# Score matmuls in four visits of four heads on four banks, values and denominators together, VectorE's steps in other slots

## The chip, the cores and the metric

One core of a Trainium2 chip runs the whole kernel. The metric is the device time of one execution in microseconds (us).

## The reference

The input x (32 batches of 256 tokens, 256 features) passes three blocks, each followed by a residual and a norm. The first, four layers of a recurrence, takes the first 2150 us and isn't touched. The second and third are "the second stage":

```python
q, k, v = heads(x @ Wq), *heads(context @ Wkv)          # 16 heads of 64
sim = clip(where(mask, q k^T * SCALE, -max), -5, 5)
x = layernorm(x + softmax(sim) v @ Wo + bo)
gate = silu(bitlinear(x, w_gate)); up = bitlinear(x, w_up)
x = layernorm(x + bitlinear(gate * up, w_down))         # INNER 1024
# bitlinear: activations rounded to 127 steps of the row's maximum, weights to -1, 0, 1
```

Ahead of them the first block's output gets its norm, is added to x and normed again: this is "the norm of the later batch" below (`x1_...`), since it is made two batches ahead.

## The kernel before, in words

`attend_and_feed` is the second stage. Each engine has its own instruction list, written out by hand in a loop over the 32 batches `j`; they meet at semaphores alone. PSUM has eight banks of 128 x 512 float32. In batch `j` the engines make the attention of `j`, the feed-forward of batch `f = j - 1`, and on VectorE the norms of batch `later = j + 2`.

TensorE's list for a batch: twelve `unit`s (L844, L851: the projections to k, q and v, in a high and a low half-precision part; 8 to 11 are v), with `transpose_x` and `feed_in` of `f` between them; `scores(j, pair)` (L866: two heads, six matmuls of 64 rows each, the two heads side by side in the array). Then four quads `q` of four heads: `attend(j, q, half)` (L876: values, 32 columns at a time), `denominators(j, q)` (L888), `out_project` (L920), and once a batch `x1_features(j + 1)` (L911), `transpose_h(f)` (L957), `feed_out(f)` (L966).

Who serves the scores: VectorE clips each head from PSUM to `scores` (`clip`, L1184); ACT exponentiates (`exps`, L1036); POOL adds the two halves of the keys (`add_halves`, L780), and among these additions splits the context of batch `j + 2` (`context_split`, L766, L768) after the fourth and makes `attended_lo` (L784). `denominators` sums over partitions; ACT takes logarithm and reciprocal (`denominators`, L1080, L1082); VectorE multiplies (`attended`, L1269); ACT makes the high part (`attended_hi`, L1089), POOL, or in the last quad VectorE (`last_attended_lo`, L1276), the low part, for `out_project`.

VectorE has besides: `h_max`, `h_steps`, `h_round_up` (L1236), `h_round_down` (L1240), which quantise the hidden values of `f` in two tiles of 128 tokens; `fed` (L1282) and the sum `x_plus_attended` (L1472). For the later batch it has `x1_moments(later, 0)` (L1296, L1299), `x1_centre` (L1305), `x1_residual` (L1314), `x1_moments(later, 1)`, `x1_second_norm` (L1324). After each pair of moments ACT makes the reciprocal deviation: `x1_rstd` (L1093, L1095), which in ACT's list of quads 2 and 3 stands right ahead of `denominators(j, q)`:

```python
                for q in range(QUADS):
                    for i in range(4 * q + 4, 4 * q + 8):
                        if i == 4 * q + 6:
                            if q > 1 and later:
                                x1_rstd(later, q - 2)
                            denominators(j, q)
                        if i < AHEADS:
                            exps(j, i)
```

`h_features` (L1059) on ACT copies the transposed hidden values for `feed_out`. Three banks (0 to 2) hold scores, 3 and 4 values and denominators (and units), 5 the output, 6 and 7 the feed-forward and the transposed `x1`.

## Time and profile before

| | us |
|---|---|
| median of 3 runs (lowest to highest) | 3659.48 (3659.18 to 3664.34) |
| the profiled execution | 3659.03 |
| its span | 3657.3 |
| TensorE busy, matmuls | 3537.8 (97%) |
| VectorE busy | 3376.8 (92%) |
| ACT busy | 3049.9 (83%) |
| POOL busy | 2178.4 (60%) |

Busy time on TensorE counts matmuls whose ends are modelled, so that 97% is not 97% of what the array can do. The span has two parts: up to 2148 us the recurrence, then the second stage. An engine's list runs strictly in order, so the time at which an instruction starts is set by the one ahead of it or by the last semaphore that it waits for; the views in order of time show which, in brackets behind the row.

### The profile page before, as it was taken

The page shows a single profiled execution, that of the slowest core. Times are in us where ns is not written, and L with a number is a line of the kernel's source. Part 1 is how long each engine was busy: PE and PEld are TensorE (multiplying, and loading weights), DVE is VectorE, ACT ScalarE, POOL GpSimd, SP SyncE. Part 2 cuts the span into 40 slices and gives each one's busy share as a digit, 9 for nine tenths or more (in the row PEclk, how much of TensorE's full clock was granted, in tenths as well). Part 3 has the DMA queues.
Part 4 walks back from the last instruction along what each step waited for, and adds up shares of the span by engine and source line. Part 5 has one row for each costly group of instructions (what it writes and reads, how often), then busy time and mean ns, then how long its engine had stood idle before and what let it go on. Part 6 is the DMA issues. An engine that isn't in the chain of part 4 may idle for free. (4 is left out here: it accounts for less than half of the span.)

```text
span 3657.3 us, 168844 instructions
## 1 busy us (share of the span) xinstructions
PE 3537.8 (97%) x71457; PEld 2324.8 (64%) x71489; DVE 3376.8 (92%) x9520; ACT 3049.9 (83%) x6636; POOL 2178.4 (60%) x2395
## 2 busy tenths in 40 slices
PE   5999999999999999999999978999999999999997
PEld 3666666666666666666666645666666666666664
DVE  8999999999999999999999988898898888888986
ACT  4999999999999999999999965777776777767765
POOL 3777777777777777777777736444444444444442
PEclk9999999999999999999999988999999999999998
DMA  2000222101000100011000100000000000000000
GB/s 83 25 26 26 57 60 55 26 26 26 25 26 26 27 25 26 25 27 26 25 26 25 27 27 10 25 25 28 31 26 25 25 25 25 25 25 25 25 16 10
DMA packets 99981, 104.36 MB, mean 29 GB/s; under 512 B 17296, under 2 KB 95004, under 8 KB 98728
## 3 DMA queue, kind: packets, MB, share of 16 engines
q1 hardware_dynamic: 99224, 93.56, 8.9%
q8 instruction: 562, 9.21, 1.0%
q14 instruction: 195, 1.60, 0.1%
HBM read 48.52 MB, written 17.53 MB: 18 GB/s over the span
## 5 line engine op out<-in xcount | busy, mean ns | idle before, releaser
L572 POOL TENSOR_TENSOR conv_products<-normed_features,conv_taps_by_token 128x256 f32<-128x256 f32 (+1 forms) x837 | 757.2, 919 | 599.9 <-ACT normed_features L355 419.7
L780 POOL TENSOR_TENSOR exps_of_both_halves<-scores 128x256 f32<-128x256 f32 x512 | 424.7, 852 | 582.5 <-ACT scores L1036 577.1
L299 PE MATMUL banks<-up_centred,after_cell_features 128*32 128x336 f32 x8928 | 684.1, 446 | 4.9 <-DVE after_cell L534 4.9
L299 PEld LDWEIGHTS banks<-up_centred,after_cell_features 128*32 128x32 f32 x8928 | 302.3, 109 | 300.9 <-issue 244.3
L306 PE MATMUL banks<-down,hidden_features 112*32 112x256 f32 x6696 | 421.0, 383 | 0.3 <-DVE growth L518 0.3
L1036 ACT ACTIVATE scores<-scores 128x512 f32<-128x512 f32 x512 | 305.8, 627 | 76.2 <-DVE scores L1184 72.8
L394 ACT ACT_TABLE_LOAD x279 | 358.0, 1283 | 5.0
L373 ACT ACT_TABLE_LOAD x279 | 358.0, 1283 | 4.9
L585 POOL TENSOR_TENSOR conv_partial_sums<-conv_products,conv_partial_sums 128x512 f32<-128x512 f32 x279 | 358.8, 1286 | 0.0
L1184 DVE SCALAR_TENSOR_TENSOR scores<-banks,score_top 128x512 f32<-128x512 f32 x512 | 328.0, 682 | 26.4 <-PE banks L866 26.1
L273 PE MATMUL banks<-recurrent_weights,h_features 64*32 64x256 f32 x8928 | 313.8, 380 | 0.0
L876 PE MATMUL banks<-scores,v_tokens 128*32 128x256 f32 x4096 | 273.6, 385 | 12.6 <-ACT scores L1036 12.4
L306 PEld LDWEIGHTS banks<-down,hidden_features 112*32 112x32 f32 x6696 | 190.5, 109 | 121.9 <-issue 1.9
L534 DVE SCALAR_TENSOR_TENSOR after_cell<-banks,rstd,layer_inputs 128x64 f32<-128x64 f32 x1116 | 237.1, 272 | 1.6 <-PE banks L292 0.9
L582 POOL TENSOR_TENSOR conv_partial_sums<-conv_products,conv_partial_sums 128x256 f32<-128x256 f32 x279 | 218.4, 783 | 0.0
L590 POOL TENSOR_TENSOR conv_partial_sums<-conv_products,conv_partial_sums 128x256 f32<-128x256 f32 x279 | 204.4, 733 | 21.9
L273 PEld LDWEIGHTS banks<-recurrent_weights,h_features 64*32 64x32 f32 x8928 | 202.5, 106 | 6.3 <-issue 0.4
L844 PE MATMUL banks<-batch_inputs_hi,qkv_weights_hi 128*128 128x256 f16 x1024 | 196.1, 273 | 9.4 <-POOL batch_inputs_lo L768 8.0
L844 PE MATMUL banks<-batch_inputs_hi,qkv_weights_lo 128*128 128x256 f16 x1024 | 196.0, 273 | 0.0
L844 PE MATMUL banks<-batch_inputs_lo,qkv_weights_hi 128*128 128x256 f16 x1024 | 195.9, 273 | 0.0
L876 PEld LDWEIGHTS banks<-scores,v_tokens 128*32 128x32 f32 x4096 | 120.8, 110 | 108.0 <-ACT scores L1036 27.9
L273 PE MATMUL banks<-gate_weights,convolved_features 64*32 64x128 f32 x8928 | 186.6, 276 | 0.0
(221 smaller groups left out, 9781.0 us busy)
## 6 DMA issues: line engine op xcount, KB each, us to landing
layer_inputs<-layer_outputs SPq DMA_DIRECT2D x279, 96.0 KB, 2.0
layer_inputs<-in_x SPq DMA_DIRECT2D x280, 32.0 KB, 1.7
x_scratch<-layer_outputs SPq DMA_DIRECT2D x279, 32.0 KB, 2.1
x_tokens<-in_x SPq DMA_DIRECT2D x32, 256.0 KB, 3.0
context_features<-in_ctx SPq DMA_DIRECT2D x32, 256.0 KB, 3.7
layers_out<-x_scratch SPq DMA_DIRECT2D x32, 256.0 KB, 2.8
out<-result SPq DMA_DIRECT2D x64, 128.0 KB, 1.8
up_centred<-in_ff_up SPq DMA_DIRECT2D x1, 2688.0 KB
```

Of the source, the lines that this page charges most:

```text
L273: mm = nc.tensor.matmul(bank[group(l), 2 * (j % 2) + odd, at + g0 * DH:at + g1 * DH], src[r, n, group(l)], w[r, l, n, g0:g1, :].rearrange( ...
L299: mm = nc.tensor.matmul(bank[group(l), b, 0:UP], xmt[:, n, group(l)], up[:, l, n, at:at + UP], start=n == 0, stop=n == HALF - 1, skip_grou ...
L306: mm = nc.tensor.matmul(bank[group(l), FD, 0:D], hidt[:, i, group(l)], down[:, l, i, :], start=i == 0, stop=i == UTILES - 1, skip_group_ch ...
L373: nc.scalar.preload_act_table_set(LOG_EXP)
L394: nc.scalar.preload_act_table(ACT.Gelu)
L572: return nc.gpsimd.tensor_tensor(prod[:, i:i + n], xnt[:, j % NRING].rearrange("p n t -> p (n t)")[:, None, :].broadcast_to([P, n, HALF * ...
L585: nc.gpsimd.tensor_tensor(new[:, 0:2], prod[:, 0:2], old[:, 1:3], ALU.add).then_inc(conv_done, 1)
L780: nc.gpsimd.tensor_tensor(psum[:, i % RING, :], pr[:, i % RING, 0:S], pr[:, i % RING, S:2 * S], ALU.add).then_inc(halves_added, 1)
L844: mm = nc.tensor.matmul(bank[:, b, i * S:(i + 1) * S], w_[:, m, h, (2 * n + i) * P:(2 * n + i + 1) * P], x_[:, j % SLOTS, src, h, :], star ...
L876: mm = nc.tensor.matmul(bank[32 * g:32 * g + 32, b, at:at + S], stationary(kt, i), pr[:, i % RING, kt * S:(kt + 1) * S], start=kt == 0, st ...
L1036: nc.scalar.activation(pr[:, i % RING, :], pr[:, i % RING, :], ACT.Exp, scale=S_SCALE).then_inc(exp_done, 1)
L1184: nc.vector.scalar_tensor_tensor(out=pr[:, i % RING, :].rearrange("p (k s) -> p k s", k=KT), in0=bank[:, i % SCORES, :].rearrange("p (k s) ...
```

## The change

Scores get a fourth bank, 6, and `scores(j, q)` makes two pairs in one visit: four visits a batch where there were eight. The second pair of a visit uses banks 2 and 6, and waits for the gate of `f` (read from bank 6) or for the clips of two pairs earlier. In each quad `attend`, `denominators` and `attend` now follow each other. `x1_features` moves behind them, to bank 7. `transpose_h` and `h_features` are done in two halves: tile 0 at the end of quad 2, tile 1 in quad 3, and both `feed_out` behind the quads. On VectorE all four clips of a quad stand ahead of `attended`; `h_max` of the last round comes ahead of the first clips; the steps of the quantisation and of the later batch's norm get other slots. No instruction is added or left out in a steady batch.

```diff
-    SCORES, UBANKS, OUTB, FFB = 3, 5, 5, 6
-    AV, DEN = SCORES, SCORES + 1
+    AV, DEN, UBANKS, OUTB, FFB = 3, 4, 5, 5, 6
+    ROWB = FFB + 1
+    SCORE_BANKS = (0, 1, 2, FFB)
+    UNIT_SCORES = 3
...
-            def scores(j, pair):
-
-                if pair == 0:
-                    pe.wait_ge(lo_done, SPLIT * (j + 1))
-                else:
-                    pe.wait_ge(clip_done, AHEADS * j + 2 * pair - 1)
-                for kt in range(KT):
-                    for part, (k_, q_) in enumerate(((k_hi, q_hi), (k_lo, q_hi), (k_hi, q_lo))):
-                        for hh in range(2):
-                            r = slice(ADH * hh, ADH * (hh + 1))
-                            mm = nc.tensor.matmul(bank[:, (2 * pair + hh) % SCORES, kt * S:(kt + 1) * S],
-                                                  k_[r, pair, kt * P:(kt + 1) * P], q_[r, pair, :], start=part == 0, stop=part == 2)
-                            if kt == KT - 1 and part == 2:
-                                mm.then_inc(s_ready, 1)
+            def scores(j, q):
+
+                for pair in (2 * q, 2 * q + 1):
+                    if pair == 0:
+                        pe.wait_ge(lo_done, SPLIT * (j + 1))
+                    elif pair == 1 and j > 0:
+                        pe.wait_ge(gate_done, ROUNDS * j)
+                    elif pair > 1:
+                        pe.wait_ge(clip_done, AHEADS * j + 2 * pair - 2)
+                    for kt in range(KT):
+                        for part, (k_, q_) in enumerate(((k_hi, q_hi), (k_lo, q_hi), (k_hi, q_lo))):
+                            for hh in range(2):
+                                r = slice(ADH * hh, ADH * (hh + 1))
+                                mm = nc.tensor.matmul(bank[:, SCORE_BANKS[2 * (pair % 2) + hh], kt * S:(kt + 1) * S],
+                                                      k_[r, pair, kt * P:(kt + 1) * P], q_[r, pair, :], start=part == 0, stop=part == 2)
+                                if kt == KT - 1 and part == 2:
+                                    mm.then_inc(s_ready, 1)
...
             def x1_features(n):
                 pe.wait_ge(x1_step, X1_OPS * (n + 1))
+                if n == 1:
+                    pe.wait_ge(ff_op, 1)
                 if n > 1:
                     pe.wait_ge(h_done, ROUNDS * (n - 1))
                 for h in range(HALF):
                     for tt in range(QT):
-                        mm = nc.tensor.transpose(bank[:, FFB, h * S + tt * P:h * S + (tt + 1) * P], x1[:, tt, h * P:(h + 1) * P], identf[:])
+                        mm = nc.tensor.transpose(bank[:, ROWB, h * S + tt * P:h * S + (tt + 1) * P], x1[:, tt, h * P:(h + 1) * P], identf[:])
...
+            def transpose_h(j, tt):
+                pe.wait_ge(hquant_step, h_quantised(j, tt))
+                if tt == 0 and j + 2 < B:
+                    pe.wait_ge(x1_split, j + 3)
+                if tt == 1 and j + 1 < B:
+                    pe.wait_ge(clip_done, AHEADS * (j + 2))
...
                 scores(0, 0)
                 pe.wait_ge(ff_parts, 3)
-                nc.tensor.matmul(bank[:, FFB + 1, 0:3], onesf[:], ff_part[:], start=True, stop=True).then_inc(ff_sums, 1)
-                scores(0, 1)
+                pe.wait_ge(x1_split, 1)
+                nc.tensor.matmul(bank[:, ROWB, 0:3], onesf[:], ff_part[:], start=True, stop=True).then_inc(ff_sums, 1)
...
+                    unit(j, SPLIT + 1)
                     scores(j, 0)
-                    unit(j, SPLIT + 1)
-                    scores(j, 1)
                     unit(j, SPLIT + 2)
                     unit(j, SPLIT + 3)
                 for q in range(QUADS):
                     if q + 1 < QUADS:
-                        scores(j, 2 * q + 2)
+                        scores(j, q + 1)
+                    attend(j, q, 0)
+                    denominators(j, q)
+                    attend(j, q, 1)
                     if q == 0 and j + 1 < B:
                         x1_features(j + 1)
-                    attend(j, q, 0)
-                    if q + 1 < QUADS:
-                        scores(j, 2 * q + 3)
-                    denominators(j, q)
-                    attend(j, q, 1)
-                    if q == 2 and j > 0:
-                        transpose_h(f)
                     if q == 3 and j > 0:
-                        feed_out(f)
+                        transpose_h(f, 1)
                     if q > 0:
                         out_project(j, 2 * q - 2)
                         out_project(j, 2 * q - 1)
+                    if q == 2 and j > 0:
+                        transpose_h(f, 0)
+                if j > 0:
+                    feed_out(f, 0)
+                    feed_out(f, 1)
                 out_project(j, APAIRS - 2)
...
-                        h_features(f)
+                    if q > 1 and j > 0:
+                        h_features(f, q - 2)
...
-                        if r + 1 < ROUNDS:
-                            h_max(f, r)
+                        h_max(f, r)
                     for i in range(4):
                         clip(j, i)
-                if j > 0:
-                    h_max(f, ROUNDS - 1)
                     h_steps(f)
-                    h_round_up(f, 0)
-                for s_ in range(2 * QUADS):
-                    q = s_ // 2
+                for q in range(QUADS):
                     if q + 1 < QUADS:
-                        clip(j, 2 * s_ + 4)
-                        clip(j, 2 * s_ + 5)
-                    if s_ % 2 and q + 1 < QUADS:
+                        for i in range(4 * q + 4, 4 * q + 8):
+                            clip(j, i)
+                    if q == 1 and j + 1 < B:
+                        x1_lo(j + 1)
+                    if q + 1 < QUADS:
                         attended(j, q)
-                    if s_ == 2 and j + 1 < B:
-                        x1_lo(j + 1)
                     if j > 0:
-                        if s_ == 0:
+                        if q == 0:
+                            h_round_up(f, 0)
+                        if q == 1:
                             h_round_down(f, 0)
-                        if s_ == 1:
+                        if q == 2:
                             h_round_up(f, 1)
-                        if s_ == 2:
                             h_round_down(f, 1)
+                    if j == 0 and q > 0:
+                        ternary(q - 1)
                     if later:
-                        if s_ == 3:
+                        if q == 1:
                             x1_moments(later, 0)
-                        if s_ == 4:
+                        if q == 2:
                             x1_centre(later)
-                        if s_ == 5:
+                        if q == 3:
                             x1_residual(later)
-                        if s_ == 6:
                             x1_moments(later, 1)
-                        if s_ == 7:
-                            x1_second_norm(later)
-                    if j == 0 and s_ in (3, 5, 7):
-                        ternary(s_ // 2 - 1)
                 attended(j, QUADS - 1)
                 last_attended_lo(j)
+                if later:
+                    x1_second_norm(later)
```

Also changed alike: `feed_out(j, tt)`, `h_features(j, tt)`, `fed`, `x1_hi`, `x1_lo` and the sums of `ff` use `ROWB` (7) and `ROWB - tt`; `unit` waits with `UNIT_SCORES`; `clip` reads `SCORE_BANKS[i % 4]`.

**VectorE, second half of a batch.** Before, from the clips behind `x1_moments(later, 0)` to `attended` and `attended_lo` of the last quad (`layers_out` and `x_tokens` are the later batch's):

```order
L1184 SCALAR_TENSOR_TENSOR scores<-banks,score_top 128x512 x2
L1305 SCALAR_TENSOR_TENSOR layers_out<-layers_out,x_mean_var,post_scale 128x256 x2
L1184 SCALAR_TENSOR_TENSOR scores<-banks,score_top 128x512 x2
L1269 TENSOR_TENSOR attended<-banks,denominator_log 128x512
L1314 SCALAR_TENSOR_TENSOR x_tokens<-layers_out,x_rstd,x_tokens 128x256 x2
L1296 BN_STATS x_bn_stats<-x_tokens 128x6 x2
L1299 BN_AGGR x_mean_var<-x_bn_stats 128x2 x2
L1324 TENSOR_SCALAR x_tokens<-x_tokens,x_mean_var,x_rstd 128x256 x2
L1269 TENSOR_TENSOR attended<-banks,denominator_log 128x512
L1276 TENSOR_TENSOR attended_lo<-attended,attended_hi 128x512
```

Now, from `attended` of quad 2 (the first row) on, with the line numbers of the changed file, which are 9 higher:

```order
L1278 TENSOR_TENSOR attended<-banks,denominator_log 128x512
L1245 TENSOR_SCALAR gate<-hidden_f,quant_scale 128x1024
L1249 TENSOR_SCALAR hidden_quant<-gate 128x1024
L1314 SCALAR_TENSOR_TENSOR layers_out<-layers_out,x_mean_var,post_scale 128x256 x2
L1323 SCALAR_TENSOR_TENSOR x_tokens<-layers_out,x_rstd,x_tokens 128x256 x2
L1305 BN_STATS x_bn_stats<-x_tokens 128x6 x2
L1308 BN_AGGR x_mean_var<-x_bn_stats 128x2 x2
L1278 TENSOR_TENSOR attended<-banks,denominator_log 128x512
L1285 TENSOR_TENSOR attended_lo<-attended,attended_hi 128x512
L1333 TENSOR_SCALAR x_tokens<-x_tokens,x_mean_var,x_rstd 128x256 x2
```

Both rounding steps of tile 1 and `x1_centre` now stand between `attended` of quad 2 and the second moments; `x1_second_norm` has gone behind the last subtraction.

**ACT, end of a batch.** Before, from the exponentials of the last two heads on:

```order
L1036 ACTIVATE scores<-scores 128x512 x2
L1089 ACTIVATE attended_hi<-attended 128x512
L1059 ACTIVATE hidden_features<-banks 128x1024 x2
L1093 ACTIVATE x_log_rstd<-x_mean_var,eps 128x2
L1095 ACTIVATE x_rstd<-x_log_rstd 128x2
L1080 ACTIVATE denominator_log<-banks 128x256
L1082 ACTIVATE denominator_log<-denominator_log 128x256
L1089 ACTIVATE attended_hi<-attended 128x512
```

Now:

```order
L1045 ACTIVATE scores<-scores 128x512 x2
L1097 ACTIVATE attended_hi<-attended 128x512
L1067 ACTIVATE hidden_features<-banks 128x1024
L1101 ACTIVATE x_log_rstd<-x_mean_var,eps 128x2
L1103 ACTIVATE x_rstd<-x_log_rstd 128x2
L1088 ACTIVATE denominator_log<-banks 128x256
L1090 ACTIVATE denominator_log<-denominator_log 128x256
L1097 ACTIVATE attended_hi<-attended 128x512
L1067 ACTIVATE hidden_features<-banks 128x1024
```

The second copy of `hidden_features` stands behind the last `attended_hi`; the later batch's `x_rstd` stays ahead of the last denominators.

**TensorE, quad 0 to quad 1.** Before, the second pair of heads for quad 2, between values and denominators of quad 1 (the six rows of L866 are one visit):

```order
L876 MATMUL banks<-scores,v_tokens 32x256 x8
L866 MATMUL banks<-q_hi,k_hi 128x256 x2
L866 MATMUL banks<-q_hi,k_lo 128x256 x2
L866 MATMUL banks<-q_lo,k_hi 128x256 x2
L866 MATMUL banks<-q_hi,k_hi 128x256 x2
L866 MATMUL banks<-q_hi,k_lo 128x256 x2
L866 MATMUL banks<-q_lo,k_hi 128x256 x2
L888 MATMUL banks<-exps_of_both_halves,ones_for_sums 32x256 x4
L876 MATMUL banks<-scores,v_tokens 32x256 x8
```

Now values, denominators and values of quad 1 in a row:

```order
L871 MATMUL banks<-q_hi,k_lo 128x256 x2
L871 MATMUL banks<-q_lo,k_hi 128x256 x2
L881 MATMUL banks<-scores,v_tokens 32x256 x8
L893 MATMUL banks<-exps_of_both_halves,ones_for_sums 32x256 x4
L881 MATMUL banks<-scores,v_tokens 32x256 x8
L927 MATMUL banks<-wo_hi,attended_hi 128x256
L927 MATMUL banks<-wo_lo,attended_hi 128x256
```

The scores stand ahead of all three, so `denominators(j, 1)` follows `attend(j, 1, 0)` at once.

## Rows read from the trace of the kernel before

**Rows 1.** The page, share of each engine in the span.
```profile
PE 3537.8 (97%) x71457; PEld 2324.8 (64%) x71489; DVE 3376.8 (92%) x9520; ACT 3049.9 (83%) x6636; POOL 2178.4 (60%) x2395
```

**Rows 2.** `x_plus_attended`, one pair a batch: ns min/median/max, count, first and last start.
```profile
L1472 DVE SCALAR_TENSOR_TENSOR x_plus_attended<-banks,x_plus_bo x64: 414/420/425, 2236.5 to 3625.1; 128x256 f32<-128x256 f32 x64
```

**Rows 3.** Order of time on TensorE: start us, us, line, names, count [idle before <-releaser].
```profile
3021.17 0.28 PE L866 MATMUL banks<-q_hi,k_hi 64*128 64x256 f16 x2
...
3021.93 0.64 PE L888 MATMUL banks<-exps_of_both_halves,ones_for_sums 128*32 128x256 f32 x8
...
3024.56 1.07 PE L876 MATMUL banks<-scores,v_tokens 128*32 128x256 f32 x16 [0.37 <-ACT scores L1036]
...
3026.32 0.64 PE L888 MATMUL banks<-exps_of_both_halves,ones_for_sums 128*32 128x256 f32 x8
...
3036.56 0.61 PE L888 MATMUL banks<-exps_of_both_halves,ones_for_sums 128*32 128x256 f32 x8
...
3037.97 1.92 PE L966 MATMUL banks<-ff_ternary,hidden_features 128*128 128x256 bf16 x16
...
3042.35 0.38 PE L844 MATMUL banks<-batch_inputs_hi,qkv_weights_hi 128*128 128x256 f16 x2
```

**Rows 4.** The same batch on POOL.
```profile
3018.82 1.95 POOL L780 TENSOR_TENSOR exps_of_both_halves<-scores 128x256 f32<-128x256 f32 x2 [0.81 <-ACT scores L1036]
...
3022.86 3.33 POOL L780 TENSOR_TENSOR exps_of_both_halves<-scores 128x256 f32<-128x256 f32 x4
...
3034.32 1.60 POOL L780 TENSOR_TENSOR exps_of_both_halves<-scores 128x256 f32<-128x256 f32 x2 [0.75 <-ACT scores L1036]
```

**Rows 5.** The same batch on ACT.
```profile
3027.03 0.39 ACT L1080 ACTIVATE denominator_log<-banks 128x256 f32<-128x256 f32 x1 [0.26 <-PE banks L888]
...
3028.49 1.23 ACT L1036 ACTIVATE scores<-scores 128x512 f32<-128x512 f32 x2 [0.62 <-DVE scores L1184]
...
3035.35 1.92 ACT L1059 ACTIVATE hidden_features<-banks 128x1024 bf16<-128x1024 bf16 x2
...
3037.16 0.29 ACT L1093 ACTIVATE x_log_rstd<-x_mean_var,eps 128x2 f32<-128x2 f32 x1
...
3037.99 0.42 ACT L1082 ACTIVATE denominator_log<-denominator_log 128x256 f32<-128x256 f32 x1
...
3039.17 0.63 ACT L1089 ACTIVATE attended_hi<-attended 128x512 f16<-128x512 f32 x1 [0.76 <-DVE attended L1269]
```

**Rows 6.** The same batch on VectorE.
```profile
3027.78 1.28 DVE L1184 SCALAR_TENSOR_TENSOR scores<-banks,score_top 128x512 f32<-128x512 f32 x2
...
3028.98 0.68 DVE L1269 TENSOR_TENSOR attended<-banks,denominator_log 128x512 f32<-128x512 f32 x1
...
3031.63 1.35 DVE L1305 SCALAR_TENSOR_TENSOR layers_out<-layers_out,x_mean_var,post_scale 128x256 f32<-128x256 f32 x2
...
3034.10 0.68 DVE L1269 TENSOR_TENSOR attended<-banks,denominator_log 128x512 f32<-128x512 f32 x1
...
3034.70 1.51 DVE L1314 SCALAR_TENSOR_TENSOR x_tokens<-layers_out,x_rstd,x_tokens 128x256 f32<-128x256 f32 x2
```

**Rows 7.** The rounding steps of 1,024 values, 2300 to 3600 us: ns min/median/max.
```profile
L1236 DVE TENSOR_SCALAR gate<-hidden_f,quant_scale x58: 743/753/1177, 2302.3 to 3561.5; 128x1024 f32<-128x1024 f32 x58
...
L1240 DVE TENSOR_SCALAR hidden_quant<-gate x58: 684/1110/1251, 2304.4 to 3564.4; 128x1024 bf16<-128x1024 f32 x58
```

**Rows 8.** Order of time on VectorE in batch 0, POOL idle beside it.
```profile
2191.19 0.88 DVE L1314 SCALAR_TENSOR_TENSOR x_tokens<-layers_out,x_rstd,x_tokens 128x256 f32<-128x256 f32 x2
```

**Rows 9.** Stretches of TensorE: from:to us, PE busy us (count), granted clock, DMA.
```profile
2204.72:2206.64 1.92, 0.01 (x2) 1.00 0.02 4
...
2208.42:2213.47 5.05, 5.05 (x36) 0.50 0.00 0
...
2215.51:2217.35 1.84, 0.00 (x1) 1.00 0.00 0
...
2166.49:2169.10 2.61, 2.61 (x7) 0.50 0.00 0
```

More of the change, by code:

```diff
@@ L1028, in _ @@
                 feed_in(f, r)
-            transpose_h(f)
-            feed_out(f)
+            for tt in range(QT):
+                transpose_h(f, tt)
+            for tt in range(QT):
+                feed_out(f, tt)
         @block.scalar
@@ L1173, in _ @@
             nc.scalar.preload_act_table_set(LOG_EXP)
-            h_features(f)
+            for tt in range(QT):
+                h_features(f, tt)
             rstds(f, zmv_done, zrstd_step, zmv, zlrstd, zrstd)
```

50 lines of the change are left out of this document (21 added, 29 removed).

## The prediction

> **What bounds the kernel now.** Read the profile in this order. First the engines' shares: TensorE 97%, VectorE 92% [rows 1]; neither has room. Then what repeats: one pair of `x_plus_attended` per batch, the first at 2236.5 us and the last at 3625.1, so 31 batches in 1388.6 us, **44.8 us each** [rows 2]. Whatever the change does, it does 31 times or so; 0.2% of the kernel (7.3 us, about what a measurement can tell from no change) is only 0.24 us a batch. Then TensorE's order of time in one batch [rows 3]: it hardly stops. What it loses is 0.37 us at 3024.56, where it waits for the exponentials, and some 0.1 us at each change between score matmuls (64 rows of the array) and others: the six pairs of a visit, at the 0.11 us that each start follows the one before, are 0.65 us, and 3021.17 to 3021.93 is 0.76. Then POOL, ACT and VectorE of the same batch [rows 4 to 6]: each is a queue in fixed order, and its place in the batch is what I follow below. All times are microseconds of this batch; the next one's units start on TensorE at 3042.35 [rows 3].
>
> **What TensorE gains.** Eight visits to the scores become four, so some eight changes go: 8 x 0.11 = 0.9 us. The waits for clips and exponentials inside the visits go too (0.37 of it is the row above), at most 0.7 more. If nothing new stood in the way, a batch would be 0.9 to 1.6 us shorter, 28 to 50 us over 31.
>
> **What takes it back: POOL first.** `denominators(j, 1)` waits for eight additions of POOL. Before, it started at 3026.32 [rows 3], just after they ended at about 3026.15. Now no score visit stands between values and denominators, and TensorE would reach it at 3026.32 - 0.37 - 6 x 0.11, about 3025.3. But POOL's four additions take 3.3 us and stand behind the split of a later batch's context, which stands behind additions 2 and 3 [rows 4]. These start 0.70 after the exponentials; those come 0.3 us earlier, because the first scores are made in one visit, ahead of unit 10. So POOL is ready 0.3 earlier and no more, and denominators(1) starts at **3026.04**, 0.28 earlier than before. Three quarters of TensorE's lead is gone here.
>
> **Then VectorE, in its new order.** The clips of four heads stand together, ahead of `attended(j, q)`, and that one waits for the denominator; behind it are now the quantisation and the norm of the later batch. I lay it out from 3026.04 with the rows' prices:
> - denominators(1) at 3026.04; its logarithm 0.71 later [rows 3, 5], the reciprocal 0.42 and its end 0.42 after that, so attended(1) at 3027.67 (before 3028.98 [rows 6]; VectorE stands idle for it about 0.9 us, its four clips and x1_lo being done).
> - attended 0.61, h_round_down(0) 1.16 (1.25 with POOL at work [rows 7], less the 0.09 by which the next one overlaps it), x1_moments(later, 0) 0.87: 3030.31. The moments' price is 3034.70 to 3037.16, less the 1.51 of the residual and 0.08 of latency [rows 5, 6].
> - The clips of the last four heads start at 3030.31, not at the 3029.7 when their scores are there. A clip is 0.60 (two in 3027.78 to 3028.98). The second starts at 3030.91, its exponential 0.72 later [rows 5, 6] and takes 0.52 of the queue, the first rstd 0.42: logarithm of denominators(2) at 3032.57, reciprocal at 3032.97, attended(2) at **3033.47**, 0.63 ahead of before [rows 6]. So far the change leads.
> - But before, only x1_residual and x1_moments(1) stood between attended(2) and the rstd that ACT makes ahead of the last denominator: 3034.10 to 3037.16. Now it is attended 0.60, h_round_up(1) 0.70 (0.75 less the overlap, and a little for POOL [rows 7]), h_round_down(1) 1.16, x1_centre 1.18 (1.27 in the queue before, all of it beside POOL [rows 6]), x1_residual 0.80, moments and latency 0.95: 5.39 us, so the rstd starts at **3038.86**, 1.70 late.
>
> The residual is 0.80 and not 1.43 because POOL will have stopped: two residuals took 1.51 us beside POOL's additions [rows 4, 6] and 0.88 where POOL stood still [rows 8]. Here the Trainium skill (SBUF — State Buffer, Who interferes with whom) states that VectorE instructions with two SBUF inputs and GpSimd lock each other out of one pair of ports; by that rule, the trace agrees. Were the residual at its old price, the batch would be 0.63 longer, which is in the upper bound.
>
> **ACT passes the delay on.** In ACT's queue the second rstd of the later batch stands ahead of the denominators of quad 3, then come attended_hi(3) and, new, `h_features(f, 1)`, which before was done with (f, 0) at 3035.35. From rstd to attended_hi is 2.01 us (3037.16 to 3039.17 [rows 5]): 3040.87. It holds the queue 0.54, the copy takes half of 1.92: 3042.37, and feed_out(f, 1) starts at 3042.47. TensorE would be there at 3039.8: attend(3, 0) at about 3034.5, denominators(3) behind POOL's last additions (1.60 after 3034.0, so 3035.7 [rows 4]), with the values behind them 1.4 (3036.56 to 3037.97 [rows 3]), half of the transposes 0.46, two pairs of projection 1.3, feed_out(f, 0) 0.88. It **stands still for 2.7 us**, once a batch. Behind it are half of what 3037.97 to 3042.35 holds [rows 3], 2.19 us: the next batch starts at 3044.66, against 3042.35. **+2.3 us a batch.**
>
> Bounds: with the least of h_round_up and h_round_down, 0.66 and 0.60 [rows 7], and x1_centre at the residual's undisturbed 0.80, the stretch of 5.39 is 4.41: +1.3. With the most of both, 1.09 and 1.16 [rows 7], and 1.27 and 1.43 for the norm's two it is 6.5: +3.4. Batches 1 to 29 have both a later batch and a feed-forward: 29 x 2.3 = 67 us (38 to 99). Batches 30 and 31 have no later norm and keep part of the gain, together -1. Batch 0 and the end: the same work in slightly other places, 0 (-3 to +3). `x1_second_norm`, moved behind the last subtraction, costs nothing: VectorE waits for feed_out there.
>
> **The clock.** A stand of 2.7 us is of the kind after which TensorE's clock has fallen in this trace. TensorE stopped at 2204.72 and went on at 2208.42; the granted clock was full (2.4 GHz) for the first 1.92 of these 3.70 us, fell, and the engine then worked 5.05 us at half of it (1.2 GHz). After another stand it worked 2.61 us at 1.2 GHz; a stand of 1.84 us passed with the clock up [rows 9]. 2.7 lies between 1.84 and 3.7, nearer the middle; I take that the clock falls in two of three batches, and that half of 2.6 to 5.1 us is lost each time, 1.9 us, for the matmuls behind it are dense: 29 x 2/3 x 1.9 = **37 us**; ends 0 and 29 x 2.55 = 74. The Trainium skill (TensorE: Matmul & The Clock Gate, HAM oscillation — how this bites in real kernels) goes further: a wait that recurs in every tile takes the clock down in every tile. By it the sum would hold the 74 and not the 37. No steady batch of this trace has such a stand, so no row here shows it.
>
> **Sum.** The profiled execution took 3659.03 us, with its span of 3657.3; the runs' median is 3659.48, so both stand for the same kernel. 3659 + 67 + 37 - 1 = **3762 us**.
>
> **Rivals.**
> 1. The same lateness, but the clock stays up: 3659 + 66 = 3725. For it: the one stand under 2 us passed, and if the stretch is nearer its lower bound the stand is not much longer. It differs from the forecast in size only.
> 2. The clock falls in every batch, as the skill's rule has it: 3659 + 66 + 74 = 3799.
> 3. **Faster:** VectorE is not late. This needs the stretch between attended(2) and the second rstd to end before 3037.2, so under 3.7 us where I have 5.4 and a lower bound of 4.4. Then TensorE's own order decides, POOL's wait included: the lead at feed_out is about 0.4 us (3039.3 would be the old place of its last 1.3, 38.9 the new), 31 x 0.4 = 12: 3647; with POOL's wait gone as well, 3659 - 40 = 3619. Against it: the four pieces are on VectorE in any case and it has 92% [rows 1].
> 4. The order does not bite because ACT or VectorE makes up the time elsewhere: gain and delay cancel, 3659. The lead of 0.63 at attended(2) is the most I find.
>
> **How the numbers follow.** Forecast 0.50, rival 1 0.25, rival 2 0.13, rival 3 0.07, rival 4 0.05, of which 0.03 falls within 0.2% and 0.01 on each side. Faster 0.08, same 0.03, slower 0.89. The range leaves out rivals 3 and 4 and reaches from 3659 + 38 to 3659 + 99 + 67: 3700 to 3825.
>
> **What would show it.** Right: in a steady batch TensorE idles 2 to 3.5 us ahead of the second half of `feed_out`, put down to ACT; ACT idles some 3 us ahead of the rstd, put down to VectorE; the batch is 46 to 49 us; the granted clock dips at batch ends. POOL is named ahead of the second denominators. Wrong: no idle time at feed_out, a batch of 44.5 or less, or the delay found at the clips instead.

## The result and the profile after

The changed kernel takes **3792.14 us** (median of 4 runs, 3786.64 to 3795.45) against 3661.02 (4 runs, 3659.18 to 3664.34) for the kernel before on the same chip: ratio **1.0355, 95% interval 1.0343 to 1.0367**, slower by 131 us. The forecast was 3762 us in a range of 3700 to 3825. The profiled execution took 3786.64 us, its span is 3784.9.

The page of the changed kernel, share of each engine in the span (before: [rows 1]):

```profile
PE 3571.1 (94%) x71457; PEld 2371.6 (63%) x71489; DVE 3406.2 (90%) x9520; ACT 3042.6 (80%) x6636; POOL 2157.8 (57%) x2395
```

TensorE's instructions are the same in number, yet it is busy 33 us longer: the same matmuls at a lower clock. Its share fell all the same, so it also stands still where it did not. `x_plus_attended`, one pair a batch, ns min/median/max (before: [rows 2]):

```profile
L1476 DVE SCALAR_TENSOR_TENSOR x_plus_attended<-banks,x_plus_bo x64: 414/420/426, 2239.9 to 3752.5; 128x256 f32<-128x256 f32 x64
```

1512.6 us for 31 batches where there were 1388.6: +124 of the 128 us between the two profiled executions lie in the steady batches, 3.4 ahead of the first. TensorE in order of time (before: [rows 3]), start, duration, line, names, [idle before <-releaser]. Its units of this batch start at 2976.49, those of the next at 3025.89:

```profile
3004.06 0.61 PE L893 MATMUL banks<-exps_of_both_halves,ones_for_sums 128*32 128x256 f32 x8
...
3014.14 0.64 PE L893 MATMUL banks<-exps_of_both_halves,ones_for_sums 128*32 128x256 f32 x8 [0.35 <-POOL exps_of_both_halves L782]
...
3017.34 1.04 PE L973 MATMUL banks<-ff_ternary,hidden_features 128*128 128x256 bf16 x8
3021.64 1.89 PE L973 MATMUL banks<-ff_ternary,hidden_features 128*128 128x256 bf16 x8 [3.27 <-ACT hidden_features L1067]
```

The second half of `feed_out` starts 3.27 us after TensorE is done with the first. The same eight matmuls take 1.04 us ahead of that stand and 1.89 behind it. The stretches of TensorE around it (from:to us, PE busy, PEld, DVE, ACT, POOL, granted clock, DMA; before: [rows 9]):

```profile
3017.34:3018.38 1.04, 1.04 (x10) 0.69 (x7) 0.66 (x4) 0.31 (x2) 0.00 (x0) 1.00 0.00 0
3018.38:3021.64 3.26, 0.00 (x0) 0.00 (x1) 1.62 (x4) 2.42 (x5) 0.00 (x0) 0.87 0.00 0
3021.64:3026.30 4.66, 4.66 (x22) 3.30 (x23) 2.33 (x9) 0.50 (x2) 0.00 (x0) 0.50 0.01 2
3026.30:3028.00 1.70, 1.70 (x12) 1.28 (x10) 1.46 (x6) 0.00 (x0) 0.97 (x1) 0.61 0.00 0
3028.00:3032.00 4.00, 4.00 (x39) 3.58 (x38) 3.08 (x10) 3.39 (x6) 0.30 (x1) 1.00 0.00 0
```

The granted clock falls from its full 2.4 GHz to 1.2 within the stand and, in this batch, stays there for some six microseconds of dense matmuls. Who waits for whom, 2500 to 3500 us (us in total, times, longest):

```profile
ACT x_log_rstd L1101 <- DVE x_mean_var L1308: 78.9, 20, 4.0
...
PE banks L973 <- ACT hidden_features L1067: 65.3, 20, 3.3
```

So TensorE waits for ACT, and ACT for VectorE's moments, once in each batch. VectorE from the clips of quad 2 on (before: [rows 6]):

```profile
3003.21 2.47 DVE L1193 SCALAR_TENSOR_TENSOR scores<-banks,score_top 128x512 f32<-128x512 f32 x4
...
3006.20 0.68 DVE L1278 TENSOR_TENSOR attended<-banks,denominator_log 128x512 f32<-128x512 f32 x1
...
3011.66 0.69 DVE L1278 TENSOR_TENSOR attended<-banks,denominator_log 128x512 f32<-128x512 f32 x1 [0.64 <-ACT denominator_log L1090]
3012.26 1.23 DVE L1245 TENSOR_SCALAR gate<-hidden_f,quant_scale 128x1024 f32<-128x1024 f32 x1
3013.53 1.10 DVE L1249 TENSOR_SCALAR hidden_quant<-gate 128x1024 bf16<-128x1024 f32 x1
3014.55 1.78 DVE L1314 SCALAR_TENSOR_TENSOR layers_out<-layers_out,x_mean_var,post_scale 128x256 f32<-128x256 f32 x2
3016.25 0.87 DVE L1323 SCALAR_TENSOR_TENSOR x_tokens<-layers_out,x_rstd,x_tokens 128x256 f32<-128x256 f32 x2
```

ACT (before: [rows 5]) and POOL (before: [rows 4]) of the same batch:

```profile
3018.04 0.30 ACT L1101 ACTIVATE x_log_rstd<-x_mean_var,eps 128x2 f32<-128x2 f32 x1 [3.95 <-DVE x_mean_var L1308]
...
3020.05 0.63 ACT L1097 ACTIVATE attended_hi<-attended 128x512 f16<-128x512 f32 x1 [0.76 <-DVE attended L1278]
3020.58 1.01 ACT L1067 ACTIVATE hidden_features<-banks 128x1024 bf16<-128x1024 bf16 x1
```

```profile
2997.46 1.41 POOL L782 TENSOR_TENSOR exps_of_both_halves<-scores 128x256 f32<-128x256 f32 x2 [0.36 <-ACT scores L1045]
2998.82 0.61 POOL L768 CAST batch_inputs_hi<-context_features 128x512 f16<-128x512 f32 x1
2999.51 1.16 POOL L770 TENSOR_TENSOR batch_inputs_lo<-context_features,batch_inputs_hi 128x512 f16<-128x512 f32 x1
3000.64 3.24 POOL L782 TENSOR_TENSOR exps_of_both_halves<-scores 128x256 f32<-128x256 f32 x4
...
3012.22 1.86 POOL L782 TENSOR_TENSOR exps_of_both_halves<-scores 128x256 f32<-128x256 f32 x2 [0.84 <-ACT scores L1045]
3014.04 1.61 POOL L786 TENSOR_TENSOR attended_lo<-attended,attended_hi 128x512 f16<-128x512 f32 x1
```

ACT stands 3.95 us ahead of the second `rstd` with the denominators of quad 3, `attended_hi` and the copy queued behind it. On POOL, two additions take 1.41 us early in the batch and 1.86 beside VectorE's rounding steps; `attended_lo` takes 1.61 beside `x1_centre`.

**The sum of it.** Between successive `x_plus_attended`, 5 of the 29 batches that have a later norm and a feed-forward take 47.35 us, those in which the clock stayed up; the other 24 take 48.6 to 50.7. Against 44.79 before, the lateness is 2.56 a batch, 29 x 2.56 = 74 us. All 29 together exceed 29 x 47.35 by 53 us: 1.4 of it belongs to the first batch whatever the clock (experiment 3 has it too), the rest is the clock, 2.2 us on average in each of the 24. The loss in a batch has two sizes: from the start of `feed_out`'s second half to the first half of the next batch TensorE takes 43.05 us with the clock up, 1.3 to 1.7 more in 13 of the 24, and 2.7 to 2.9 more in the other 11, in which the granted clock stayed low twice as long. The two batches without a later norm give back 3.7, the start adds 3.4. 74 + 53 - 3.7 + 3.4 = 127 of 128 us.

### The profile page after: what moved, and what is told of

The parts are those of the page before. It is cut to its first block and busy times, and to the rows that moved or that the text cites. A ratio compares the mean times of both kernels' runs of the same rounds, so it can differ in the third digit from the quotient of the medians.

```text
span 3784.9 us, 168877 instructions
## 1 busy us (share of the span) xinstructions
PE 3571.1 (94%) x71457; PEld 2371.6 (63%) x71489; DVE 3406.2 (90%) x9520; ACT 3042.6 (80%) x6636; POOL 2157.8 (57%) x2395
## 5 line engine op out<-in xcount | busy, mean ns | idle before, releaser
L782 POOL TENSOR_TENSOR exps_of_both_halves<-scores 128x256 f32<-128x256 f32 x512 | 404.2, 813 | 594.9 <-ACT scores L1045 592.3
L1193 DVE SCALAR_TENSOR_TENSOR scores<-banks,score_top 128x512 f32<-128x512 f32 x512 | 316.8, 680 | 23.6 <-PE banks L871 23.4
L776 POOL TENSOR_TENSOR x_plus_bo<-x_tokens,bo 128x512 f32<-128x512 f32 x32 | 40.6, 1268 | 360.3 <-DVE x_plus_attended L1476 324.3
```

The lines of the kernel that those rows point to most:

```text
L782: nc.gpsimd.tensor_tensor(psum[:, i % RING, :], pr[:, i % RING, 0:S], pr[:, i % RING, S:2 * S], ALU.add).then_inc(halves_added, 1)
L1193: nc.vector.scalar_tensor_tensor(out=pr[:, i % RING, :].rearrange("p (k s) -> p k s", k=KT), in0=bank[:, SCORE_BANKS[i % 4], :].rearrange( ...
```

## The experiments

The ratios are to the kernel before, run on the same chip. Differences in us to the changed kernel go across chips, whose medians of the kernel before lie between 3657.7 and 3664.5, so they are good to some 4 us. Line numbers shift by 2 or so from kernel to kernel. "A batch" is the time between successive `x_plus_attended`, for batches that have a later norm and a feed-forward; where the clock stays up, the first of these 29 is 0.6 to 1.4 us longer than the others.

**1. Only ACT's order: the last denominators ahead of the second rstd.** This cuts the chain at the place that the prediction names.

```diff
                         if i == 4 * q + 6:
-                            if q > 1 and later:
-                                x1_rstd(later, q - 2)
+                            if q == 2 and later:
+                                x1_rstd(later, 0)
                             denominators(j, q)
+                            if q == 3 and later:
+                                x1_rstd(later, 1)
```

> Only ACT's list changes: in quad 3 the logarithm and reciprocal of the denominators stand ahead of the later batch's second rstd. Theory A (VectorE's new order makes the second moments late, and ACT's order passes that on to the last denominators): the last attended then waits for VectorE alone and starts 1.3 us earlier; TensorE's stand ahead of feed_out(f, 1) shrinks from 3.27 to about 1.95 us, a batch with the clock up from 47.35 to 46.05 us, and such a stand should seldom take the clock down: 3659 + 29 x 1.26 = 3695 us, at most 3757 if the clock falls in every batch. Rival B (the visits of four heads cost the time themselves, by late clips or banks): nothing at the end of the batch matters, 3785 to 3795 us.

3693.10 us (3690.66 to 3695.49), ratio 1.0078 (1.0063 to 1.0093): 99 us less than the changed kernel, as Theory A had it. The granted clock is 1.00 over the steady part, a batch takes 45.96. TensorE's stand has become:

```profile
3019.41 1.05 PE L973 MATMUL banks<-ff_ternary,hidden_features 128*128 128x256 bf16 x8 [1.87 <-ACT hidden_features L1067]
```

A stand of 1.87 us in every batch never brought the clock down. Of the 2.56 us by which a batch was late, 1.4 come from ACT's queue order. Three quarters of the whole loss go with that order, about half of it as clock.

**2. Only the second copy earlier.** `h_features(f, 1)` goes ahead of the second rstd, so that `feed_out` no longer waits; the chain over rstd and denominators stays.

```diff
                         if i == 4 * q + 6:
+                            if q == 3 and j > 0:
+                                h_features(f, 1)
                             if q > 1 and later:
                                 x1_rstd(later, q - 2)
...
-                    if q > 1 and j > 0:
-                        h_features(f, q - 2)
+                    if q == 2 and j > 0:
+                        h_features(f, 0)
```

> Only ACT's list changes: the second copy of the hidden features stands ahead of the later batch's second rstd, in time that ACT idles away now. Theory A: feed_out(f, 1) no longer waits; TensorE stands some 2.3 us ahead of the last projection instead, for the last attended_lo, and the next batch starts 1.07 us earlier with the clock up: 46.3 us a batch, 3702 us without a fall of the clock, 3744 with a fall in two of three batches. Rival B: 3785 to 3795 us.

3751.85 us (3750.0 to 3754.12), ratio 1.0238 (1.0223 to 1.0254): above the 3744 that Theory A gave for a fall in two of three batches, and below Rival B's 3785 to 3795. The stand moved, as it should, behind `feed_out`, to the last projection:

```profile
2999.92 1.91 PE L973 MATMUL banks<-ff_ternary,hidden_features 128*128 128x256 bf16 x16
3004.03 0.40 PE L927 MATMUL banks<-wo_hi,attended_hi 128*128 128x256 f16 x1 [2.20 <-DVE attended_lo L1287]
```

A batch takes 47.9 to 48.1 in most cases, 46.29 in three, as Theory A has it with the clock up. So a stand of 2.2 us still brings the clock down, in 26 of 29 batches; the miss is that the clock was expected to stay up more often. Behind `feed_out` the stand is 1.07 us shorter, and 40 of the 131 us are won; the other 1.5 us of lateness and most falls of the clock are left.

**3. The clock alone.** 26 matmuls with no use for their results (added work, into a bank that is overwritten afterwards) fill the stand; nothing else changes.

```diff
                     feed_out(f, 0)
+                    if j + 1 < B:
+                        for _ in range(26):
+                            nc.tensor.matmul(bank[:, 0, 0:S], w_hi[:, 0, 0, 0:P], w_hi[:, 0, 0, 0:S], start=True, stop=True)
                     feed_out(f, 1)
```

> Twenty-six additional matmuls (256 columns, half precision, into a bank that nobody reads before it is overwritten) stand between the two halves of feed_out and take 2.8 of the 3.27 us for which TensorE stands still; nothing else changes and the result is the same. Theory C (the clock's fall after the stand is what makes 49.5 us out of 47.35 in 24 of 29 batches): every batch is 47.35 us, granted clock full, 3659 + 29 x 2.56 - 1 = 3732 us. Against C: the longer batches have another cause, 3785 us or more.

3739.45 us (3738.84 to 3740.89), ratio 1.0205 (1.0190 to 1.0220). A batch takes 47.35, exactly the five undisturbed ones of the changed kernel, and the granted clock is 1.00 throughout the steady part. 3792.1 - 3739.5 = **52.7 us is the price of the clock** across the two chips. Taken as what each kernel exceeds the one before on its own chip, 131.1 and 74.9, it is 56. The traces put it at 52: between the first and the last `x_plus_attended` lie 1512.3 us in the changed kernel and 1463.5 here, and 2.8 of the 1463.5 are the added matmuls in batch 30, which has no stand to fill (45.93 us, 43.09 without them). These 2.8 are also part of the 7 us by which the time is above the 3732 expected. What is left is the price of the lateness, 29 x 2.56 = 74 us.

**4. POOL's part in VectorE's stretch.** The stretch from `attended(2)` to the second rstd is 6.38 us (3011.66 to 3018.04) where the prediction had 5.39. Here POOL's work beside it is cut to one column:

```diff
             def add_halves(j, i):
...
-                nc.gpsimd.tensor_tensor(psum[:, i % RING, :], pr[:, i % RING, 0:S], pr[:, i % RING, S:2 * S], ALU.add).then_inc(halves_added, 1)
+                n_ = 1 if j > 0 and i >= AHEADS - 2 else S
+                nc.gpsimd.tensor_tensor(psum[:, i % RING, 0:n_], pr[:, i % RING, 0:n_], pr[:, i % RING, S:S + n_], ALU.add).then_inc(halves_added, 1)
```

and `attended_lo` of quad 2 alike. The other columns are left out, so part of the denominators and of the low part is stale: the run is for its times alone.

> The changed kernel, with POOL's work beside VectorE's stretch cut to one column from batch 1 on: the additions of the last two heads and the subtraction attended_lo of quad 2 (their other columns are left out, so part of the denominators and of the low part is stale). TensorE, ACT and VectorE do exactly what they did. Theory S (the stretch from attended(2) to the second rstd is 6.38 us and not 5.39 because POOL works beside h_round_up(1), h_round_down(1) and x1_centre): they fall to their undisturbed prices, 0.75, 0.68 and about 0.9, the stretch to some 4.4, the stand ahead of feed_out(1) from 3.27 to 1.3 us, the clock stays up, and a batch takes 45.4 us: 3660 to 3680 in all. Rival (the three cost what they cost because of their own order in VectorE's queue, not because of POOL): the stretch stays above 6 us, the stand above 2.8, the time within 0.3% of the changed kernel, 3780 to 3800.

3715.55 us (3714.72 to 3716.09), ratio 1.0145 (1.0128 to 1.0162). VectorE, in order of time:

```profile
3023.61 0.69 DVE L1280 TENSOR_TENSOR attended<-banks,denominator_log 128x512 f32<-128x512 f32 x1 [0.64 <-ACT denominator_log L1092]
3024.21 0.75 DVE L1247 TENSOR_SCALAR gate<-hidden_f,quant_scale 128x1024 f32<-128x1024 f32 x1
3024.99 0.69 DVE L1251 TENSOR_SCALAR hidden_quant<-gate 128x1024 bf16<-128x1024 f32 x1
3025.60 0.87 DVE L1316 SCALAR_TENSOR_TENSOR layers_out<-layers_out,x_mean_var,post_scale 128x256 f32<-128x256 f32 x2
```

1.23, 1.10 and 1.78 us have become 0.75, 0.69 and 0.87: theory S holds, the stretch is 4.57 (3023.61 to 3028.18). The time came out 36 us above its range all the same, and TensorE shows why:

```profile
3028.73 1.04 PE L975 MATMUL banks<-ff_ternary,hidden_features 128*128 128x256 bf16 x8
3031.79 1.50 PE L975 MATMUL banks<-ff_ternary,hidden_features 128*128 128x256 bf16 x8 [2.02 <-ACT hidden_features L1069]
```

The stand is 2.02 us, not 1.3: TensorE, which no longer waits for POOL at the last denominators either, starts the first half of `feed_out` 0.56 earlier (5.12 after `attended(2)` starts, in the changed kernel 5.68). And at 2.02 us the clock falls in two of three batches, 19 of 29: from one `feed_out` to the next it is 45.54, 47.22, 47.21 us in turn. The 45.54 are the expected 45.4; the other 1.68, in two thirds of 29 batches, are 32 us.

**5. One rounding step moved beside POOL's early additions.** `h_round_up(f, 0)` goes ahead of the clips of quad 1, where it stood before the change. This tests why the POOL term of the prediction did not show: TensorE was to wait there for `denominators(j, 1)`.

```diff
                 for q in range(QUADS):
+                    if q == 0 and j > 0:
+                        h_round_up(f, 0)
                     if q + 1 < QUADS:
                         for i in range(4 * q + 4, 4 * q + 8):
                             clip(j, i)
...
                         if q == 0:
-                            h_round_up(f, 0)
```

> The changed kernel with h_round_up(f, 0) put back to where it stood before, right behind h_steps and beside POOL's additions 2 and 3. Theory P (these additions took 1.95 us before because VectorE worked from SBUF to SBUF beside them, and take 1.41 now because it idles there; that is why denominators of quad 1 did not wait for POOL as I had forecast): the pair takes 1.7 to 1.95 us again and TensorE waits 0.3 to 0.9 us ahead of these denominators; the time stays within 0.3% of the changed kernel's, since VectorE has the step off its back later. Against P: 1.41 us and no wait.

```profile
3033.01 1.86 POOL L782 TENSOR_TENSOR exps_of_both_halves<-scores 128x256 f32<-128x256 f32 x2 [0.36 <-ACT scores L1045]
```

The two additions went from 1.41 to 1.86 us, as expected, towards what they took before the change [rows 4]. The rest missed: the next four took 2.80 instead of 3.24 us, with VectorE's step no longer beside them. So all eight ended as in the changed kernel, 4.12 us behind the start of `denominators(j, 0)` in both kernels, and TensorE did not wait at `denominators(j, 1)`. And the time is 3758.28 us (3756.98 to 3759.57, 2 runs), ratio 1.0274 (1.0253 to 1.0294), by the ratios 0.8% less than the changed kernel where at most 0.3% was expected. TensorE's quad 3 shows where that lies:

```profile
3048.01 1.07 PE L881 MATMUL banks<-scores,v_tokens 128*32 128x256 f32 x16
3048.92 0.64 PE L893 MATMUL banks<-exps_of_both_halves,ones_for_sums 128*32 128x256 f32 x8
```

From the denominators of quad 0 on (3035.31 here, 2999.76 in the changed kernel) those of quads 1 and 2 come at the same distances, 4.30 and 9.43 us, in both. Those of quad 3 come at 13.61 instead of 14.38: VectorE, without a rounding step in quad 0, starts the last four clips 0.80 earlier (7.99 against 8.79), so the waits for exponentials and for POOL in quad 3 are gone. 29 x 0.77 = 22 us; the stand at `feed_out` stays 3.27. The profiled executions differ by some 27 us; of the last 5, 1.6 lie ahead of the first `x_plus_attended` and 0.3 in the last batch. The clock falls here in all 29 batches, with the same stand at which it fell in 24 of the changed kernel, yet costs about the same in all: measured from 43.05 - 0.77 us, most falls cost 1.3 to 1.7 us and five 2.3 to 2.9, some 50 us together as an estimate.

**6. The order that the theory asks for.** `attended(3)` goes right behind `x1_centre` on VectorE, the rest of the norm behind it, and on ACT the second rstd goes last.

```diff
-                        if q == 3:
-                            x1_residual(later)
-                            x1_moments(later, 1)
                 attended(j, QUADS - 1)
+                if later:
+                    x1_residual(later)
                 last_attended_lo(j)
                 if later:
+                    x1_moments(later, 1)
                     x1_second_norm(later)
...
-                            if q > 1 and later:
-                                x1_rstd(later, q - 2)
+                            if q == 2 and later:
+                                x1_rstd(later, 0)
                             denominators(j, q)
...
+                    if q == 3 and later:
+                        x1_rstd(later, 1)
```

> VectorE makes the last attended right behind x1_centre, then the residual, the last attended_lo, the second moments and the second norm; ACT makes the last denominators, attended_hi and the second copy first and the later batch's second rstd behind them. Nothing of the visits, banks or the clips changes. Theory A: the last attended starts at about 3016.3 and not 3019.3 in the batch that begins at 2976.5, TensorE stands less than 1 us and the clock stays up, a batch is 44.2 to 44.8 us: 3642 to 3660 us, so the loss is gone and a small gain may be left. Rival B: above 3700 us.

**3648.00 us** (3645.52 to 3648.86), ratio 0.9953 (0.9936 to 0.9969): below the kernel before. A batch takes 44.49. What is left of TensorE's waits:

```profile
3030.29 1.07 PE L881 MATMUL banks<-scores,v_tokens 128*32 128x256 f32 x16 [0.17 <-ACT scores L1045]
3031.70 0.64 PE L893 MATMUL banks<-exps_of_both_halves,ones_for_sums 128*32 128x256 f32 x8 [0.34 <-POOL exps_of_both_halves L782]
...
3034.90 1.04 PE L973 MATMUL banks<-ff_ternary,hidden_features 128*128 128x256 bf16 x8
3036.13 1.05 PE L973 MATMUL banks<-ff_ternary,hidden_features 128*128 128x256 bf16 x8 [0.19 <-ACT hidden_features L1067]
```

**7. Is it the order alone?** The kernel before, with the same end of the batch (norm behind `attended(3)`, second rstd last) and its eight visits.

```diff
-                        if s_ == 5:
-                            x1_residual(later)
-                        if s_ == 6:
-                            x1_moments(later, 1)
-                        if s_ == 7:
-                            x1_second_norm(later)
                 attended(j, QUADS - 1)
+                if later:
+                    x1_residual(later)
                 last_attended_lo(j)
+                if later:
+                    x1_moments(later, 1)
+                    x1_second_norm(later)
```

> The kernel before, with the same new order of VectorE's and ACT's last steps as in the run that put the norm last, and with its eight visits and three banks kept. Theory A1 (the gain of that run over before comes from the four visits, which take TensorE's changes and waits away): before, TensorE did not wait at a batch's end, so there is nothing to gain; VectorE now idles between the attended of quads 2 and 3 and is later at x_plus_attended: 44.8 to 45.8 us a batch, 3658 to 3690 us. Rival D (that order alone is the gain, whatever the visits): 44.5 us a batch, 3650 us.

3677.85 us (3677.33 to 3679.39), ratio 1.0053 (1.0036 to 1.0070), as Theory A1 had it and not Rival D; a batch takes 45.34, a few 45.9. The same order costs the kernel with eight visits 0.5 us a batch and leaves the one with four 0.3 below before. The difference, 45.34 - 44.49 = 0.85 us a batch, is what the rest of the change gains, waits included: the four visits with their fourth bank, but also the new slots of the clips and of the rounding steps. No run takes these apart.

**8. And the rounding steps one slot earlier each** (6 with 5: `h_round_up(f, 0)` ahead of quad 1's clips, `h_round_down(f, 0)` in quad 0, `h_round_up(f, 1)` in quad 1, `h_round_down(f, 1)` in quad 2).

> The run that put the norm last, and besides each rounding step one slot earlier: h_round_up(f, 0) ahead of the clips of quad 1, h_round_down(f, 0) behind attended of quad 0, h_round_up(f, 1) in quad 1, h_round_down(f, 1) in quad 2. VectorE idles 0.74 us ahead of those clips in that run, so quad 2 has 1.2 us less in front of the last attended. Theory A: the last attended starts 0.5 us earlier (then the last denominators set it), 44.0 to 44.3 us a batch, 3635 to 3645 us. Against it: POOL's slower additions cost as much, 3645 to 3655 us.

**3622.46 us** (3621.23 to 3622.98), ratio **0.9902** (0.9887 to 0.9917), better than expected: 1.0% faster than before, 4.4% faster than the changed kernel. A batch takes 43.65, and TensorE no longer stands at `feed_out` at all; its largest wait is

```profile
3004.51 0.64 PE L893 MATMUL banks<-exps_of_both_halves,ones_for_sums 128*32 128x256 f32 x8 [0.16 <-POOL exps_of_both_halves L782]
```

## Why the prediction came out as it did

The sign, the mechanism and the place were right; 131 us came where 103 were forecast, and the two big terms were both too small. With the batch laid on the same zero (start of the units on TensorE, 2997.57 in the prediction's batch, 2976.49 here):

| us from the start of the units | predicted | measured |
|---|---|---|
| denominators(1) start | 28.47 | 27.57 |
| attended(1) | 30.10 | 29.71 |
| attended(2) | 35.90 | 35.17 |
| second rstd | 41.29 | 41.55 |
| attended_hi(3) | 43.30 | 43.56 |
| TensorE free for feed_out(1) | 42.2 | 41.89 |
| feed_out(1) | 44.90 | 45.15 |
| next batch, clock up | 47.09 | 47.35 |

- **"POOL first": wrong.** Denominators(1) were to start 0.28 earlier than before and started 1.18 earlier. The term took POOL's durations from the old order: 1.95 for additions 2 and 3 [rows 4]. In the new order VectorE stands idle beside them and they take 1.41, the subtraction behind them 1.16. Experiment 5 put a VectorE step back beside them and got 1.86, but the four additions behind took 0.44 less and the eight ended no later: it is the sum of POOL's queue that the term had too long, not the first pair alone. The prediction applied port sharing to VectorE's residual and forgot it for POOL.
- **The stretch from attended(2) to the rstd: right in kind, 0.99 too short.** `h_round_up` at 0.70 should have been 1.23 + 0.04 of gap, `h_round_down` at 1.16 was 1.02 in the queue, `x1_centre` at 1.18 was 1.70; residual and moments were as forecast. The prediction took the median of `h_round_up` [rows 7] over from slots in which it was VectorE's step that came first. That POOL is the reason for the longer times is shown by experiment 4; who comes first, and so which of the two pays, is read from the rows below. The two errors were nearly equal and opposite at the rstd (0.73 early, 0.99 long), so +2.3 a batch stood against a measured +2.56. The forecast was nearer than its steps deserved.
- **ACT passes the delay on: right.** 2.01 us from rstd to `attended_hi` were forecast and measured; experiment 1 cut the chain there and got 1.4 us a batch and the clock back.
- **The stand: 2.7 forecast, 3.27 measured**, half from the later copy, half because TensorE came earlier.
- **The clock: 37 us forecast, 52.7 measured** (experiment 3). It fell in 24 of 29 batches, not in two of three, and cost 2.2 us each on average, not 1.9. This lies between the forecast and rival 2, whose 3799 is the nearest single number. The Trainium skill (TensorE: Matmul & The Clock Gate, HAM oscillation — how this bites in real kernels) tells of a kernel in which a wait of some 3 to 5 us in every tile takes the clock down every time. The measured stand of 3.27 us is of that size, and five batches did escape; the 2.7 us that were forecast lay below it, so the prediction took from the page more than it tells. That shorter stands bring falls too is shown by experiments 2 and 4 alone.
- **The ends: -1 forecast, -3.7 measured**, for batches 30 and 31: without the norm, 43.10 and 42.85. Before, the same two took 44.98 and 44.66. So where no norm is in the way, the change gains 1.8 to 1.9 us, more than the 0.9 to 1.6 of the prediction. The start, put at 0 (-3 to +3), cost 3.4.
- **The range** adds 67 for the clock at its upper end where its own bound is 74; with 74 it would reach 3832.
- **Rival 1 (3725)** is experiment 3, 3739 without the clock's loss. **Rival 3 (faster)** needed the stretch under 3.7 us; it was 6.4, and 4.6 with POOL's work beside it cut. It named only that one way; experiments 6 and 8 took the residual, the moments and the rstd out of the way of the last `attended` instead. Their 3648 and 3622 lie close to its 3647 and 3619, but in other orders than it was worked out for, so that is no check of its sum.

## What to carry to other kernels

When steps of a side job are moved between engines' slots, look for the instruction of the main path that is queued behind them on a third engine: here a tiny rstd ahead of the last denominators turned a late norm into a stand of TensorE, and putting the denominators ahead of it in ACT's list won back three quarters of the loss. Take the price of a VectorE or POOL instruction from a row in which the other engine does what it will do in the new slot; a median over a kernel mixes both. Count a recurring stand of the matmul engine twice, for itself and for the clock: filling it (experiment 3) won back the clock's part alone, and a stand cut to 2.2 us (experiment 2) still paid for the clock in 26 of 29 batches.

## What the runs showed of the hardware

- **How sharply the clock depends on the stand.** With one stand a batch, 1.87 us passed in all batches (experiment 1), as 1.84 had in the trace of before [rows 9]; 2.02 us brought the clock down in two of three, 2.2 us in 26 of 29, 3.27 us in 24 of 29 of the changed kernel and in all 29 of experiment 5. A stand of some 2 us had been expected to bring it down seldom. The pattern of three in experiment 4 was strikingly regular. These are different kernels with other work around the stand, and the two with the same stand of 3.27 us differ, so the length of the stand is not all of it, and no more than these six points is claimed.
- **What a fall costs:** 1.68 us behind a 2.02 us stand; behind 3.27 us, 1.3 to 1.7 in 13 falls of the changed kernel and 2.7 to 2.9 in 11. The longer price goes with a granted clock that stays low longer, not with a longer stand.
- **VectorE and POOL slow each other, one-input instructions included.** On VectorE the 1,024-element multiply-and-add took 0.75 us alone and 1.23 beside POOL, the rounding to bf16 0.69 and 1.10, the pair of two-input steps 0.87 and 1.78; POOL's pair of additions 1.41 and 1.86. In experiment 8 that pair on VectorE even took 2.26. Which of the two pays differs: in the kernel before, the same multiply-and-add began 0.08 us ahead of POOL's two additions and kept its 0.75, and they took 1.95 [rows 4]; in the changed kernel it begins 0.04 behind them and takes 1.23. Of the kernel before, and of experiment 8:

```profile
3018.74 0.75 DVE L1236 TENSOR_SCALAR gate<-hidden_f,quant_scale 128x1024 f32<-128x1024 f32 x1
```

```profile
3013.17 2.26 DVE L1316 SCALAR_TENSOR_TENSOR layers_out<-layers_out,x_mean_var,post_scale 128x256 f32<-128x256 f32 x2
```

- **Read this one instruction at a time.** A row of two or four additions hides which of them paid. In the kernel before, the next multiply-and-add stands in the middle of four additions and keeps 0.74; it began 0.08 us ahead of the third addition, and that one took 1.26 where one beside which VectorE did no such step takes 0.73:

```profile
3024.16 0.74 DVE L1236 TENSOR_SCALAR gate<-hidden_f,quant_scale 128x1024 f32<-128x1024 f32 x1
```

```profile
3024.24 1.26 POOL L780 TENSOR_TENSOR exps_of_both_halves<-scores 128x256 f32<-128x256 f32 x1
```

In the changed kernel both engines pay, each in its turn. POOL's first addition begins first and keeps 0.73, the multiply-and-add begins behind it (3012.26) and takes 1.23, the second addition begins behind that and takes 1.18, and the rounding to bf16 (3013.53) behind that takes 1.10:

```profile
3012.22 0.73 POOL L782 TENSOR_TENSOR exps_of_both_halves<-scores 128x256 f32<-128x256 f32 x1 [0.84 <-ACT scores L1045]
```

```profile
3012.91 1.18 POOL L782 TENSOR_TENSOR exps_of_both_halves<-scores 128x256 f32<-128x256 f32 x1
```

The Trainium skill (SBUF — State Buffer, Who interferes with whom) names both kinds, a VectorE instruction with two SBUF inputs and `tensor_scalar` in a mode that takes both port pairs, and says that the order of issue decides who is blocked. Experiment 4 agrees on both kinds, and the rows above agree on the order: in each pair that overlaps, it is the instruction that began second that takes longer than its shortest time.
